# A float32r attention and gated feed-forward layer on one core: V projected for two heads at a time, residual rows kept partly in DRAM

## The chip, the cores and the metric

The kernel runs on one core of a Trainium2 chip. The metric is the device time of one execution in microseconds (us); lower is better. TensorE (PE) multiplies, VectorE (DVE), ScalarE (ACT) and GpSimd (POOL) work element by element, and SyncE (SP) issues most of the DMAs; ACT issues the rest. Each engine takes its own instructions strictly in the order in which they are written, and waits on semaphores of the others.

## The reference

```python
x = L0_attn_x                       # (4, 1024, 256)
q, k, v = x @ Wq + bq, x @ Wk + bk, x @ Wv + bv     # 16 heads of 128; q scaled by 128 ** -0.5
q, k = rotary(q), rotary(k)
attn = softmax(where(causal, -max, q @ k.T))
x = layernorm(x + (attn @ v) @ Wo + bo)
gate = silu((x @ w_gate) * s_gate); up = (x @ w_up) * s_up      # int8 weights, 1024 wide
x = layernorm(x + ((gate * up) @ w_down) * s_down)
```

## The kernel before

Every float32 operand of a product is kept as two float32r parts, high and low, and a product is the sum of three: high x high, high x low, low x high. So each operand costs a copy on ACT that makes the high part, and a subtraction on DVE or POOL that makes the low part (the helper `sub`, L582, on DVE, and the helper `copy`, L402, on ACT).

The work is a sequence of 64 heads (4 batches of 16). `run(n, par, ...)` writes out the time line of head `n`; `par` is 0 for even heads and 1 for odd ones, and picks the halves A or B of the double buffers. A time line has eight slots, `s` = 0 to 7. Slot `s` computes the scores of query rows `s` (L823), masks them and takes the maximum on DVE (L670), and exponentiates on ACT (L527). Slots 0 to 3 also project Q and K of head n + 1 in four chunks of 512 columns (L866), which ACT copies out (L535), DMAs swap (L283), POOL and DVE rotate (L347, L699, L646), and ACT and POOL split (L402, L358). Every even head's slots 2 and 3 and every odd head's slots 1 and 2 carry an output projection (L903), which DVE adds to the residual rows in `resid` (L692).

Probabilities are transposed on PE (L833), and the transposed block is split by ACT and DVE into `PT` before `attend` multiplies it with V (L848 to L850). The twelve steps k of a head are spread over its slots: steps 8 to 11 over its own slots 4 to 7 and the next head's slot 0, and steps 0 to 7, whose probabilities come from slots 4 to 7, over the next head's slots 0 to 4. The transposes of steps 0 and 1 are in slot 0, and wait for the exponential of the previous head's slot 7. After step 7 DVE normalises the output from bank `O` (`norm_o`, L627).

V of head n + 1 is projected in slots 4 to 7 of head n by `v_pair`, one pair of 128-row tiles each, into bank `PJ`. A tile takes four products: two 256 columns wide, in which the high part of x meets both parts of Wv, and two 128 columns wide. ACT copies the high half (L402), DVE subtracts it (L582 into `v_rest`) and adds the cross products (L638). In slots 4 to 7 ACT's order is the V copy, the copy of `PT`, the exponential; DVE's is the mask, `norm_o` in slot 4, the two V operations, the low part of `PT`, the rotation's sum (slots 4 and 5).

`resid` holds the rows of all four batches. Behind the last head comes the feed-forward stage in eight groups of 512 rows (`group`, L774, L969), of which six are in a loop.

Of the kernel before, what the change touches and what calls it, by code (L numbers as in the profile page):

```python
# [27 lines left out]
H, D = 16, 128  # L28
# [16 lines left out]
def layer(nc, x_rows, x_cols, w_heads, bias_qk, bias_v, wo_heads, bias_o, wg8, wu8, wd8, s_gate, s_up,  # L45
# [7 lines left out]
    def sem(name):  # L53
# [3 lines left out]
    recip_d = nc.dram_tensor("recip_d", (2, GQ), F32).ap()  # L57

# [3 lines left out]
    w_raw = sb("w_raw", [P, 3, KT, P])  # L62
    wo_raw = sb("wo_raw", [P, 2, DIM])

    W = [sb(f"W{s}", [P, 3, 2, KT, P], F32R) for s in "AB"]
# [8 lines left out]
    resid = sb("resid", [P, B * NT, DIM])  # L74
# [5 lines left out]
    v_rest = sb("v_rest", [P, 2, P])  # L80
# [30 lines left out]
    v_psum = PJ[:, :].rearrange("p (t a d) -> p t a d", t=2, a=2)  # L111
# [3 lines left out]
    W_in, x_first, x_in = sem("W_in"), sem("x_first"), sem("x_in")  # L115
    WO_in = sem("WO_in")
# [6 lines left out]
    maxed, pt_lo, cos_done, rot_done, v_sub, v_lo, o_norm, recip_ok, added = (  # L123
        sem(n) for n in ("maxed", "pt_lo", "cos_done", "rot_done", "v_sub", "v_lo", "o_norm", "recip_ok", "added"))
# [25 lines left out]
    def n_w(m, q):  # L150
        return 3 * m + (q + 1)

    def n_x(b, half):
        return b * 2 + (half + 1)

# [17 lines left out]
    def timelines(e, run):  # L173


        run(-1, 1, False, False, True, False)
        run(0, 0, True, False, True, False)
        run(1, 1, True, True, True, False)
        with e.Fori(1, PAIRS - 1) as it:
            run(it * 2, 0, True, True, True, True)  # L180
            run(it * 2 + 1, 1, True, True, True, True)
        run(HEADS - 2, 0, True, True, True, True)
        run(HEADS - 1, 1, True, True, False, True)
        run(HEADS, 0, False, True, False, True)

# [3 lines left out]
    def w_piece(n, s):  # L189
        return s - (4 if isinstance(n, int) and n < 0 else 1)  # L190
# [19 lines left out]
    def sequence_timelines(e, run):  # L210


        run(-1, 1, False, False, True, False)
        run(0, 0, True, False, True, False)
        run(1, 1, True, True, True, False)
        with e.Fori(1, H // 2 - 1) as it:
            run(it * 2, 0, True, True, True, True)
            run(it * 2 + 1, 1, True, True, True, True)
        with e.Fori(0, B - 1) as b:
            last = b * H + (H - 2)  # L220
            run(last, 0, True, True, True, True, b + 1)
            run(last + 1, 1, True, True, True, True, b + 1)
            with e.Fori(1, H // 2) as it:
                first = b * H + it * 2 + (H - 2)
                run(first, 0, True, True, True, True)
                run(first + 1, 1, True, True, True, True)
        run(HEADS - 2, 0, True, True, True, True)
        run(HEADS - 1, 1, True, True, False, True)
        run(HEADS, 0, False, True, False, True)


    flat_v = [v[:, :, :, :].rearrange("p a t d -> p (a t d)") for v in V]

    ffn_w = [xT[:, a, :, :].rearrange("p t n -> p (t n)") for a in range(2)] + [flat_v[0]]
    x1T = [t.rearrange("p (a t q) -> p a t q", a=2, t=KT)
           for t in (flat_v[1], OT[0][:, :, :].rearrange("p a n -> p (a n)"))]
# [19 lines left out]
    def groups(e, run):  # L256

        run(0, 0, True, True)
        with e.Fori(0, (FG - 2) // 2) as it:
            run(it * 2 + 1, 1, False, True)  # L260
            run(it * 2 + 2, 0, False, True)
        run(FG - 1, 1, False, False)

    with nc.Block() as block:  # L264

        @block.sync
        def _(sp):
# [9 lines left out]
            def run(n, par, own, prev, project, out_proj, next_x=None):  # L277
                for s in range(8):
# [6 lines left out]
                    if isinstance(n, int) and n == 0 and s == 6:  # L285
                        for b in range(B):
                            sp.dma_start(resid[:, b * NT:(b + 1) * NT, :], x_rows[b]).then_inc(resid_in, 16)
# [761 lines left out]
```

## Time and profile before

| | |
|---|---|
| median of 3 runs | 2173.8 us (2173.39 to 2177.66) |
| the profiled execution | 2175.21 us, of which 2173.4 us is the span of its instructions |
| mean granted TensorE clock over the span | 0.988 |
| PE, DVE, ACT, POOL busy | 2089.3, 1750.5, 1416.5, 1304.1 us |
| DMA | 150.27 MB, mean 69 GB/s |
| loads of all residual rows, at head 0 | 4 of 1024 KB, median 11.3 us to landing |
| loads of x for batches 1 to 3 | 3 of 1024 KB, median 5.2 us to landing |

Busy time is the time in which an engine worked on an instruction. For PE the ends of matmuls are modelled and neighbours overlap, so a busy PE can hide short waits: the distance between the starts of neighbours tells more. A wait of an engine is shown with the instruction that ended it.

### The profile page before, as it was taken

How to read it: one execution, taken by the hardware profiler on the slowest of the kernel's cores; microseconds unless marked ns; L12 is line 12 of the kernel's file. 1: busy time of each engine (PE TensorE's matmuls, PEld its weight loads, DVE VectorE, ACT ScalarE, POOL GpSimd, SP SyncE). 2: the span in 40 equal slices, each digit the busy share in tenths (PEclk: the TensorE clock that was granted, in tenths of full speed). 3: DMA queues.
4: the chain of work that ended last, by engine and by line, in shares of the span. 5: the costliest groups of instructions: out<-in, count | busy, mean ns of one | idle time of the engine just before them, and what ended most of it. 6: DMA issues, size and time to landing. Idle time of an engine off the chain costs nothing. (4 is left out here: it accounts for less than half of the span.)

```text
span 2173.4 us, 49354 instructions
## 1 busy us (share of the span) xinstructions
PE 2089.3 (96%) x13136; PEld 1860.5 (86%) x13136; DVE 1750.5 (81%) x3547; ACT 1416.5 (65%) x3230; POOL 1304.1 (60%) x1080
## 2 busy tenths in 40 slices
PE   6999999999999999999999999999999999979997
PEld 5888888888888888888888888888888888868886
DVE  5788888888888888888888888888888888865776
ACT  4676666676666666666667666676666776654543
POOL 4566656676666666576666666675666666524554
PEclk8999999999999999999999999999999999988999
DMA  4432223233232332333222233323232223310000
GB/s 115 148 73 68 72 73 73 64 86 75 73 73 73 67 69 70 73 92 70 68 68 73 73 73 70 84 72 73 74 69 68 68 73 73 80 25 1 29 19 29
DMA packets 99871, 150.27 MB, mean 69 GB/s; under 512 B 31216, under 2 KB 35824, under 8 KB 99312
## 3 DMA queue, kind: packets, MB, share of 16 engines
q1 hardware_dynamic: 85856, 115.82, 22.2%
q10 hardware_dynamic: 13968, 33.95, 5.7%
q14 instruction: 33, 0.27, 0.1%
q8 instruction: 14, 0.23, 0.0%
HBM read 78.15 MB, written 4.46 MB: 38 GB/s over the span
## 5 line engine op out<-in xcount | busy, mean ns | idle before, releaser
L582 DVE TENSOR_TENSOR PT<-TP,PT 128x512 fp32r<-128x512 f32 (+3 forms) x768 | 421.3, 552 | 210.0 <-ACT PT L402 206.7
L527 ACT ACTIVATE prob<-prob,neg_max 128x128 f32<-128x128 f32 (+7 forms) x512 | 397.8, 777 | 288.4 <-DVE neg_max L670 280.4
L402 ACT ACTIVATE PT<-TP 128x512 fp32r<-128x512 f32 (+3 forms) x768 | 361.4, 489 | 90.3 <-PE TP L833 80.6
L670 DVE CUSTOM_DVE_ANT_0 prob<-S,mask_row 128x128 f32<-128x128 f32 (+7 forms) x512 | 380.7, 744 | 27.1 <-PE TP L833 12.4
L347 POOL TENSOR_TENSOR swap<-swap,sin_t 128x512 f32<-128x512 f32 x256 | 350.3, 1368 | 82.7 <-DMA swap<-proj 80.4
L833 PE MATMUL TP<-ident,prob 128*128 128x128 f32 x2304 | 369.4, 274 | 0.7 <-ACT prob L527 0.7
L833 PEld LDWEIGHTS TP<-ident,prob 128*128 128x128 f32 x2304 | 283.1, 141 | 55.5 <-ACT prob L527 1.1
L646 DVE TENSOR_TENSOR rot<-rot,swap 128x512 f32<-128x512 f32 x256 | 286.3, 1119 | 7.6 <-POOL swap L347 7.2
L358 POOL TENSOR_TENSOR QKB<-rot,QKB 128x512 fp32r<-128x512 f32 x128 | 171.8, 1342 | 196.1 <-ACT QKB L402 196.1
L358 POOL TENSOR_TENSOR QKA<-rot,QKA 128x512 fp32r<-128x512 f32 x128 | 182.4, 1425 | 169.1 <-ACT QKA L402 168.4
L823 PE MATMUL S<-QKB 128*128 128x512 f32 (+4 forms) x1152 | 261.2, 353 | 1.3 <-DVE resid L692 1.3
L823 PE MATMUL S<-QKA 128*128 128x512 f32 (+4 forms) x1152 | 259.9, 352 | 1.1 <-ACT proj L535 1.1
L535 ACT ACTIVATE proj<-S,bias_m 128x512 f32<-128x512 f32 x256 | 173.8, 679 | 91.1 <-DVE rot L646 89.1
L866 PE MATMUL S<-xT,WA 128*128 128x512 f32 x768 | 200.7, 398 | 8.9 <-DVE xT L582 8.9
L823 PEld LDWEIGHTS S<-QKB 128*128 128x128 f32 x1152 | 187.4, 190 | 17.9 <-issue 1.5
L823 PEld LDWEIGHTS S<-QKA 128*128 128x128 f32 x1152 | 186.9, 189 | 18.1 <-issue 1.7
L866 PE MATMUL S<-xT,WB 128*128 128x512 f32 x768 | 201.3, 397 | 0.0
L337 POOL TENSOR_TENSOR norm_o<-norm_o,bias_o_m 128x512 f32<-128x512 f32 x128 | 134.2, 1049 | 96.3 <-ACT OTA L483 67.3
L699 DVE TENSOR_TENSOR rot<-proj,cos_t 128x512 f32<-128x512 f32 x256 | 178.7, 698 | 8.0 <-ACT proj L535 8.0
L627 DVE TENSOR_TENSOR norm_o<-O,recip_b 128x512 f32<-128x512 f32 x128 | 140.4, 1097 | 40.9 <-PE O L850 40.9
L866 PEld LDWEIGHTS S<-xT,WA 128*128 128x128 f32 x768 | 140.9, 190 | 34.6 <-issue 8.9
L848 PE MATMUL O<-PT,VA 128*128 128x512 f32 (+3 forms) x384 | 141.5, 369 | 27.5 <-DVE PT L582 27.5
(107 smaller groups left out, 4722.9 us busy)
## 6 DMA issues: line engine op xcount, KB each, us to landing
swap<-proj SPq DMA_DIRECT2D x512, 128.0 KB, 2.3
recip_b<-recip_d SPq DMA_DIRECT2D x128, 256.0 KB, 3.6
w_raw<-in_w_heads ACTq DMA_DIRECT2D x65, 384.0 KB, 3.1
wo_raw<-in_wo_heads ACTq DMA_DIRECT2D x32, 256.0 KB, 3.3
resid<-in_x_rows SPq DMA_DIRECT2D x4, 1024.0 KB, 11.3
out<-resid SPq DMA_DIRECT2D x8, 512.0 KB, 3.0
x_raw<-in_x_cols SPq DMA_DIRECT2D x3, 1024.0 KB, 5.2
recip_d<-recip SPq DMA_DIRECT2D x128, 2.0 KB, 1.8
```

What stands on the lines that cost most here:

```text
L347: nc.gpsimd.tensor_tensor(swap[:, c % 2, :], swap[:, c % 2, :], sin_t[:, half], ALU.mult).then_inc(sin_done, 1)
L358: nc.gpsimd.tensor_tensor(q[:, c % 2, 1, half], rot[:, c, :], q[:, c % 2, 0, half].bitcast(F32), ALU.subtract).then_inc(rot_lo, 1)
L402: copy = lambda o, i: nc.scalar.activation(o, i, ACT.Copy)
L527: nc.scalar.activation(row, row, ACT.Exp, bias=neg_max[:, s:s + 1], scale=-1.0, accum_out=row_sum[:, s:s + 1]).then_inc(exped, 1)
L535: nc.scalar.activation(proj[:, c % 2, :], S[c % 2][:, GQ:], ACT.Identity, bias=bias_m[:, m_par, c % 2:c % 2 + 1], scale=SCALE if c % 2 == ...
L582: sub = lambda o, a, b: nc.vector.tensor_tensor(o, a, b, ALU.subtract)
L646: nc.vector.tensor_tensor(rot[:, c, :], rot[:, c, :], swap[:, c % 2, :], ALU.add).then_inc(rot_done, 1)
L670: nc.vector.tensor_tensor_reduce(row_view(prob[g][:, prob_at[g][i]:prob_at[g][i] + cols], s), score_view(S[s % 2], s), row_view(mask_row[: ...
L699: nc.vector.tensor_tensor(rot[:, c, :], proj[:, c % 2, :], cos_t[:, half], ALU.mult).then_inc(cos_done, 1)
L823: last = mm(S[s % 2][:, z * GQ:z * GQ + b - a], QK[par][:, 0, part_q, s * P:(s + 1) * P], QK[par][:, 1, part_k, a:b], start=(part_q, part_ ...
L833: last = nc.tensor.transpose(TP[k % 2][:, i * P:(i + 1) * P], prob[g][:, prob_at[g][i] + j * P:prob_at[g][i] + (j + 1) * P], ident[:, :])
L866: last = mm(S[c % 2][:, GQ:], W[nxt][:, c % 2, pw, t, :], xT[:, px, t, half], start=i == 0 and t == 0, stop=i == 2 and t == KT - 1)
```

## The change

`WV` holds the weights of two heads side by side, and `V` the values of two. V of heads n + 2 and n + 3 (n even) is now projected in slots 4 and 6 of head n and of head n + 1, one group of two row tiles each; a tile takes six products of 256 columns, and all three parts are summed in PSUM. One 512-column copy and one 512-column subtraction a group then make the two parts. In slot 4 the group stands ahead of the steps 6 and 7 on PE; on ACT its copy stands behind the exponential of the slot, and on DVE its subtraction stands behind the low part of `PT`. W is split in slots 2 and 3 instead of 1 to 3, and `WV` in slot 1 of even heads. `resid` holds two batches: one in work and a neighbour; finished rows go to `attn_d` in DRAM (1 MB a batch) and the next ones are loaded in their place, at the heads around a change of batch, where the split of the next x has moved too, to slots 2 and 5 of one head. For the feed-forward stage the rows come back into `resid` and the `prob` buffers. The attention loops are written out by four heads instead of two, and the feed-forward groups without a loop.

```diff
-    w_raw = sb("w_raw", [P, 3, KT, P])
+    w_raw = sb("w_raw", [P, 2, KT, P])
+    wv_raw = sb("wv_raw", [P, 2, KT, P])
+    WV = sb("WV", [P, 2, KT, 2, P], F32R)
-    V = [sb(f"V{s}", [P, 2, NT, P], F32R) for s in "AB"]
+    V = [sb(f"V{s}", [P, 2, NT, 2 * P], F32R) for s in "AB"]
-    resid = sb("resid", [P, B * NT, DIM])
+    resid = sb("resid", [P, 2 * NT, DIM])
+    attn_d = nc.dram_tensor("attn_d", (B, P, NT, DIM), F32).ap()
...
+    def v_group(n, par, s):
+        if isinstance(n, int) and n < 0:
+            return s - 4 if s >= 4 else None
+        return {4: 2 * par, 6: 2 * par + 1}.get(s) if makes_v(n) else None
...
@@ PE
-                        mm(v_psum[:, t2, :, :], xT[:, 0, 0, tok], w[:, :, 0, :], start=True, stop=False)
-                        for t in range(KT):
-                            mm(v_psum[:, t2, 0, :], xT[:, 1, t, tok], w[:, 0, t, :], start=False, stop=False)
-                        last = mm(v_psum[:, t2, :, :], xT[:, 0, 1, tok], w[:, :, 1, :],
-                                  start=False, stop=True)
+                        for z, (px, pw) in enumerate(((0, 0), (0, 1), (1, 0))):
+                            for t in range(KT):
+                                last = mm(v_psum[:, t2, :], xT[:, px, t, tok],
+                                          WV[:, pw, t, :, :].rearrange("p h c -> p (h c)"),
+                                          start=z == 0 and t == 0, stop=z == 2 and t == KT - 1)
...
+                    i = v_group(n, par, s)
+                    if s == 4 and i is not None:
+                        values(i)
                     if s == 4 and prev:
-                        attend(n, 6, nxt)
-                        attend(n, 7, nxt)
-                    if s == 4 and project:
-                        v_pair(0)
+                        attend(n, 6, nxt, before)
+                        attend(n, 7, nxt, before)
                     if s >= 4 and own:
                         transposes(s + 4)
-                    if s > 4 and project:
-                        v_pair(s - 4)
+                    if s > 4 and i is not None:
+                        values(i)
@@ ACT
-                    if s >= 4 and project:
-                        v = s - 4
-                        act.wait_ge(v_made, n_four(m, v))
-                        wait(act, attended, n_step(n, 7))
-                        copy(V[nxt][:, 0, 2 * v:2 * v + 2, :],
-                             v_psum[:, :, 0, :]).then_inc(v_hi, 1)
                     if s >= 4 and own:
                         probs_hi(n, s + 4)
                     if own and s >= 4:
                         softmax(n, s)
+                    i = v_group(n, par, s)
+                    if i is not None:
+                        act.wait_ge(v_made, n_v(n, par, i))
+                        if par == 0:
+                            wait(act, attended, n_step(n, 7))
+                        copy(V[1 - vb][:, 0, 2 * i:2 * i + 2, :], v_psum).then_inc(v_hi, 1)
...
+                    if next_x is not None and par == 0 and s == 0:
+                        act.wait_ge(added, n_added(n - (H - 2), 3))
+                        act.dma_start(attn_d[bass.ds((next_x + 2) & 3, 1)].rearrange("b p t c -> (b p) t c"),
+                                      half_resid(next_x)).then_inc(attn_out, 16)
+                    if next_x is not None and par == 1 and s == 3:
+                        act.wait_ge(attn_out, next_x * 16)
+                        act.dma_start(half_resid(next_x), x_rows[bass.ds(next_x, 1)].rearrange("b p t c -> (b p) t c")
+                                      ).then_inc(resid_in, 16)
+                    if isinstance(n, int) and n == HEADS - 2 and s == 6:
+                        act.wait_ge(attn_out, 16 * B)
+                        act.dma_start(resid[:, 0:NT, :], attn_d[0]).then_inc(attn_in, 16)
@@ DVE
-                    if s >= 4 and project:
-                        v = s - 4
-                        dve.wait_ge(v_hi, n_four(m, v))
-                        wait(dve, v_lo, n_four(m, v) - 1)
-                        tiles = slice(2 * v, 2 * v + 2)
-                        sub(v_rest[:, :, :], v_psum[:, :, 0, :], V[nxt][:, 0, tiles, :].bitcast(F32)
-                            ).then_inc(v_sub, 1)
-                        dve.wait_ge(v_sub, n_four(m, v))
-                        nc.vector.tensor_tensor(V[nxt][:, 1, tiles, :], v_rest[:, :, :], v_psum[:, :, 1, :],
-                                                ALU.add).then_inc(v_lo, 1)
                     if s >= 4 and own:
                         probs_lo(n, s + 4)
+                    i = v_group(n, par, s)
+                    if i is not None:
+                        dve.wait_ge(v_hi, n_v(n, par, i))
+                        tiles = slice(2 * i, 2 * i + 2)
+                        sub(V[1 - vb][:, 1, tiles, :], v_psum, V[1 - vb][:, 0, tiles, :].bitcast(F32)).then_inc(v_lo, 1)
```

PE, slot 4 of an even head in the middle of the sequence, before: the last scores, steps 6 and 7, V (PJ), the transposes of step 8.

```order
L823 MATMUL S<-QKA 128x320 x6
L845 REGISTER_ALU
L848 MATMUL O<-PT,VB 128x256
L849 MATMUL O<-PT,VB 128x256
L850 MATMUL O<-PT,VB 128x256
L848 MATMUL O<-PT,VB 128x128
L849 MATMUL O<-PT,VB 128x128
L850 MATMUL O<-PT,VB 128x128
L874 REGISTER_ALU
L878 MATMUL PJ<-WB,xT 128x256
L880 MATMUL PJ<-WB,xT 128x128 x2
L881 MATMUL PJ<-WB,xT 128x256
```

The same place of the change:

```order
L894 MATMUL S<-QKA 128x320 x6
L206 ISA
L945 ISA
L946 ISA
L951 MATMUL PJ<-WV,xT 128x256 x12
L916 REGISTER_ALU
L919 MATMUL O<-PT,VB 128x256
L920 MATMUL O<-PT,VB 128x256
L921 MATMUL O<-PT,VB 128x256
L919 MATMUL O<-PT,VB 128x128
L920 MATMUL O<-PT,VB 128x128
L921 MATMUL O<-PT,VB 128x128
```

V stood behind the six products of steps 6 and 7 and now stands ahead of them, with twelve products instead of eight. Slot 6 has the same twelve, and slots 5 and 7 none.

ACT, slot 6 of an even head, before: V (VB), the high part of PT, the exponential, a copy of the rotated rows.

```order
L402 ACTIVATE VB<-PJ 128x256
L517 REGISTER_ALU
L402 ACTIVATE PT<-TP 128x256
L524 REGISTER_ALU
L527 ACTIVATE prob,row_sum<-prob,neg_max 128x896
L402 ACTIVATE QKB<-rot 128x512
```

The same slot of the change:

```order
L447 ACTIVATE PT<-TP 128x256
L601 REGISTER_ALU
L604 ACTIVATE prob,row_sum<-prob,neg_max 128x896
L447 ACTIVATE VB<-PJ 128x512
L447 ACTIVATE QKB<-rot 128x512
```

The V copy has moved from ahead of the exponential to behind it.

DVE, slot 6 and the start of slot 7 of an even head, before: the mask, the two V operations, the low part of PT, the mask of slot 7.

```order
L670 ISA prob,neg_max<-S,mask_row 128x896
L670 ISA neg_max 128x1
L582 TENSOR_TENSOR v_rest<-PJ,VA 128x256
L638 TENSOR_TENSOR VA<-v_rest,PJ 128x256
L678 REGISTER_ALU
L582 TENSOR_TENSOR PT<-TP,PT 128x256
L619 REGISTER_ALU
L670 ISA prob,neg_max<-S,mask_row 128x1024
```

The same stretch of the change:

```order
L741 ISA prob,neg_max<-S,mask_row 128x896
L741 ISA neg_max 128x1
L749 REGISTER_ALU
L656 TENSOR_TENSOR PT<-TP,PT 128x256
L710 REGISTER_ALU
L656 TENSOR_TENSOR VB<-PJ,VB 128x512
L695 REGISTER_ALU
L741 ISA prob,neg_max<-S,mask_row 128x1024
```

One V operation is left of two, and it stands directly ahead of the mask of slot 7.

## Rows read from the trace of the kernel before

**Rows 1.** Page, part 1: busy us, share of the span, instructions.

```profile
PE 2089.3 (96%) x13136; PEld 1860.5 (86%) x13136; DVE 1750.5 (81%) x3547; ACT 1416.5 (65%) x3230; POOL 1304.1 (60%) x1080
```

**Rows 2.** Waits of PE, 100 to 1880 us: total, times, longest.

```profile
PE O L848 <- DVE PT L582: 19.8, 28, 1.0
PE PJ L878 <- DVE VA L638: 8.1, 22, 0.6
```

**Rows 3.** Timeline, PE, an odd and an even head: start, duration, count, idle before.

```profile
1012.38 1.06 PE L833 MATMUL TP<-ident,prob 128*128 128x128 f32 x8
...
1029.58 0.39 PE L848 MATMUL O<-PT,VA 128*128 128x256 f32 x1 [0.70 <-DVE PT L582]
...
1042.74 1.07 PE L833 MATMUL TP<-ident,prob 128*128 128x128 f32 x8
...
1059.10 0.28 PE L848 MATMUL O<-PT,VB 128*128 128x256 f32 x1
...
1059.74 0.33 PE L878 MATMUL PJ<-WB,xT 128*128 128x256 f32 x1
...
1060.71 0.60 PE L833 MATMUL TP<-ident,prob 128*128 128x128 f32 x4
...
1071.81 1.06 PE L833 MATMUL TP<-ident,prob 128*128 128x128 f32 x8
```

**Rows 4.** Timeline, PE, one V tile and the steps behind it.

```profile
1009.56 0.28 PE L878 MATMUL PJ<-WB,xT 128*128 128x256 f32 x1
...
1010.02 0.28 PE L848 MATMUL O<-PT,VA 128*128 128x256 f32 x1
1010.14 0.28 PE L849 MATMUL O<-PT,VA 128*128 128x256 f32 x1
```

**Rows 5.** Timeline, DVE, slots 4 to 7 of the even head.

```profile
1060.28 1.10 DVE L627 TENSOR_TENSOR norm_o<-O,recip_b 128x512 f32<-128x512 f32 x1
...
1062.13 0.68 DVE L582 TENSOR_TENSOR PT<-TP,PT 128x512 fp32r<-128x512 f32 x1
...
1062.73 0.68 DVE L646 TENSOR_TENSOR rot<-rot,swap 128x512 f32<-128x512 f32 x1
...
1063.42 0.93 DVE L670 CUSTOM_DVE_ANT_0 prob<-S,mask_row 128x768 f32<-128x768 f32 x1
...
1065.06 0.55 DVE L582 TENSOR_TENSOR PT<-TP,PT 128x384 fp32r<-128x384 f32 x1
...
1066.13 1.08 DVE L670 CUSTOM_DVE_ANT_0 prob<-S,mask_row 128x896 f32<-128x896 f32 x1
...
1068.75 1.23 DVE L670 CUSTOM_DVE_ANT_0 prob<-S,mask_row 128x1024 f32<-128x1024 f32 x1 [0.40 <-PE TP L833]
```

**Rows 6.** Timeline, ACT, same head, and the end of step 11.

```profile
1061.85 0.82 ACT L527 ACTIVATE prob<-prob,neg_max 128x640 f32<-128x640 f32 x1
...
1067.26 1.04 ACT L527 ACTIVATE prob<-prob,neg_max 128x896 f32<-128x896 f32 x1
...
1070.09 1.15 ACT L527 ACTIVATE prob<-prob,neg_max 128x1024 f32<-128x1024 f32 x1
...
1071.70 0.28 PE L850 MATMUL O<-PT,VA 128*128 128x128 f32 x1
...
1072.17 1.11 DVE L627 TENSOR_TENSOR norm_o<-O,recip_b 128x512 f32<-128x512 f32 x1 [0.82 <-PE O L850]
```

**Rows 7.** Groups by shape, 400 to 1700 us: busy us, mean ns, idle before.

```profile
L402 ACT ACTIVATE PT<-TP 128x512 fp32r<-128x512 f32 x259 | 147.6, 596 | 30.7 <-PE TP L833 24.2
```

**Rows 8.** Timeline, DVE, a rotation sum of the odd head.

```profile
1033.38 1.25 DVE L646 TENSOR_TENSOR rot<-rot,swap 128x512 f32<-128x512 f32 x1
```

**Rows 9.** Timeline, PE in the last head; busy by stretch: PE, PEld, DVE, ACT, POOL, PEclk, DMA.

```profile
1926.33 0.38 PE L848 MATMUL O<-PT,VA 128*128 128x256 f32 x1 [2.17 <-DVE PT L582]
...
1926.00:1932.00 6.00, 5.67 (x27) 5.06 (x28) 5.53 (x11) 3.35 (x6) 2.09 (x2) 0.72 0.05 16
```

**Rows 10.** Waits, 50 to 75 us: total, times, longest.

```profile
PE O L848 <- DVE PT L582: 3.6, 1, 3.6
```

More of the change, by code:

```diff
@@ L189, in w_piece @@
     def w_piece(n, s):
-        return s - (4 if isinstance(n, int) and n < 0 else 1)
+        return s - (4 if isinstance(n, int) and n < 0 else 2)
     def output_of(n, par, s, out_proj):
@@ L227, in sequence_timelines, with four @@
[L227 to L234, printed above, removed]
+        def four(first, next_x=None):
+            run(first, 0, 0, True, True, True, True)
+            run(first + 1, 1, 0, True, True, True, True)
+            run(first + 2, 0, 1, True, True, True, True, next_x)
+            run(first + 3, 1, 1, True, True, True, True, next_x)
@@ new lines, in sequence_timelines @@
+        run(-1, 1, 1, False, False, True, False)
+        run(0, 0, 0, True, False, True, False)
+        run(1, 1, 0, True, True, True, False)
+        run(2, 0, 1, True, True, True, True)
+        run(3, 1, 1, True, True, True, True)
+        with e.Fori(1, H // 4 - 1) as it:
+            four(it * 4)
+        with e.Fori(0, B - 1) as b:
+            four(b * H + (H - 4), b + 1)
+            with e.Fori(1, H // 4) as it:
+                four(b * H + it * 4 + (H - 4))
+        run(HEADS - 4, 0, 0, True, True, True, True)
@@ L254, in layer, with rows, groups @@
     DOWN_AFTER = {0: [-2], 1: [-1], 2: [], 3: [0, 1], 4: [2], 5: [3], 6: [4], 7: [5]}
[L256 to L262, printed above, removed]
+    late_rows = [p[:, 0:tiles * DIM].rearrange("p (t c) -> p t c", c=DIM) for p, tiles in ((prob[1], 12), (prob[0], 4))]
+    def rows(g, t, count=1):
+        if g < 2:
+            held = resid[:, g * TPG + t:g * TPG + t + count, :]
+        elif g < 5:
+            held = late_rows[0][:, (g - 2) * TPG + t:(g - 2) * TPG + t + count, :]
+        elif g == 5:
+            held = late_rows[1][:, t:t + count, :]
+        else:
+            held = resid[:, (g - 4) * TPG + t:(g - 4) * TPG + t + count, :]
+        return held.rearrange("p a c -> p (a c)")
+    def groups(run):
+        for g in range(FG):
+            run(g, g % 2, g == 0, g < FG - 1)
     with nc.Block() as block:
@@ L285, in run @@
                     if isinstance(n, int) and n == 0 and s == 6:
-                        for b in range(B):
+                        for b in range(2):
                             sp.dma_start(resid[:, b * NT:(b + 1) * NT, :], x_rows[b]).then_inc(resid_in, 16)
@@ L492, in run @@
                         copy(QK[nxt][:, c % 2, 0, half], rot[:, c, :]).then_inc(rot_hi, 1)
-                    if n_has(n, project) and w_piece(n, s) in range(3):
+                    if n_has(n, project) and w_piece(n, s) in range(2):
                         w_high(n + 2, par, w_piece(n, s))
+                    if par == 0 and s == 1 and own and makes_v(n):
+                        wv_high((n >> 1) + 1)
+                    if par == 0 and s == 5 and own and makes_v(n) and n_has(n + 2 if isinstance(n, int) else n, True):
+                        load_wv(n)
                     if s == 5 and n_has(n, project):
@@ L576, in group @@
                             x1T_high(g + 1, 1 - par, t)
-            groups(act, group)
+            groups(group)
         @block.vector
@@ L836, in transposes, with attend @@
                     last.then_inc(transposed, 1)
-                def attend(nn, k, who):
+                def attend(nn, k, who, buf):
                     g, j, c0 = step(k)
@@ L914, in run @@
                         output(s, *made)
+                    before = vb if par else 1 - vb
                     if prev and s == 0:
-                        attend(n - 1, 11, nxt)
+                        attend(n - 1, 11, nxt, before)
                         transposes(0)
```

201 lines of the change are left out of this document (112 added, 89 removed).

## The prediction

> **What bounds the kernel now.** I read the page first: PE is busy 96% of the span and DVE 81% [rows 1]. A busy PE can hide waits, so I looked next at who waits for whom in the steady stretch from 100 to 1880 us: PE stands still for only 28 us of 1780, nearly all of it ahead of `attend`, for DVE [rows 2]. Last I read the timeline of two neighbouring heads [rows 3]. The first transposes of slot 0 (step 0, "T0") start at 1012.38, 1042.74 and 1071.81: an odd head takes 30.36 us and an even one 29.07, 29.7 in the mean. Between them PE's instructions follow each other closely, but for the 0.70 us in slot 4 of the odd head, where step 6 waits for the low part of `PT`. So the PE is the bound, but by a narrow margin: what follows it on DVE and ACT is just in time. In the even head DVE goes from one instruction to the next from `norm_o` at 1060.28 to the mask of slot 7 at 1068.75, with an idle time of 0.40 us in those 8.5 us [rows 5]. The reader should see two chains of nearly one length in slots 4 to 7, and only PE's in slots 0 to 3.
>
> **What is taken from PE.** A V tile takes 0.46 us of PE (1009.56 to 1010.02), and products of 256 columns follow each other at 0.12 (1010.02 to 1010.14) [rows 4]. Before, a head has four groups of two tiles, about 1.0 us each (0.97 from 1059.74 to 1060.71 in [rows 3]), so 3.9. After, it has two groups of twelve products, 12 x 0.12 = 1.4, so 2.8. PE has about 1.1 us a head less to do. The odd head's 0.70 us goes too, because V now stands ahead of step 6 and fills it. If PE alone set the pace, this would be (1.1 + 0.35) x 61 heads = 88 us.
>
> **What the new order costs.** I follow the even head from the start of step 6, 1059.10 [rows 3], by distances of rows. Slots 0 to 3 hold no V; from T0 at 1042.74 to 1059.10 PE is the bound as before, 16.36 us.
> 1. V first: 1059.10 + 1.4 = 1060.5; steps 6 and 7 take 0.64 (1059.10 to 1059.74), so step 8's transposes start at 61.15, and step 7's last product at 61.05.
> 2. `norm_o` starts 0.47 behind the start of such a last product (1071.70 to 1072.17 [rows 6]): 61.52, where it was at 1060.28. DVE used to do it while PE projected V. It and its 1.1 us end at 62.6.
> 3. The exponential of slot 4 starts 1.14 behind the transposes (1060.71 [rows 3] to 1061.85 [rows 6]): 62.30, and takes 0.82. Only then comes the V copy, 0.60 for 512 columns [rows 7]: to 63.7. DVE does the low part of step 8, 0.6 (1062.13 to 1062.73 [rows 5]), to 63.2, and waits 0.6 for the copy. I give the new subtraction the same 0.6, since it reads PSUM and SBUF in the same shape: 63.8 to 64.4.
> 4. The rotation's sum and the reciprocal take 0.69 (1062.73 to 1063.42): the mask of slot 5 starts at 65.1, 1.7 later than before. It, the low part and the second rotation's sum take 0.85 + 1.07 (1065.06 to 1066.13) [rows 5]: the mask of slot 6 starts at 67.0.
> 5. The exponential of slot 6 starts 1.13 behind its mask (1066.13 [rows 5] to 1067.26 [rows 6]), and takes 1.04; the V copy 0.6; then the subtraction, 69.9 to 70.5. DVE has only the mask and a short low part, 1.4 us, to do in these 2.9, and stands idle for 1.5. Before, ACT made the V copy ahead of the exponential, and this wait wasn't there.
> 6. The mask of slot 7 stands behind it in DVE's queue: 70.5, where it was at 1068.75. Its exponential starts 1.34 later (1068.75 [rows 5] to 1070.09 [rows 6]) and takes 1.15; with 0.15 to release T0, that is 73.15. Before, T0 was at 1071.81, and V in slot 7 covered this exponential; now PE has come to the end of step 11 sooner and waits.
>
> So a head takes 16.36 + 14.05 = 30.4 us, the odd head as well, since its chain has the same parts. Against 29.7 that is +0.7, and + 0.7 x 61 = +43 us. DVE does 1.0 us a head less and loses about 2 us waiting for ACT: the saving of PE isn't used.
>
> **What else moves.** The four groups before head 0 are longer and each waits for the one before; I take +2. Two of the four residual loads are gone from head 0, behind which PE waited 3.6 us at 50 to 75 us [rows 10]: up to -3.6, I take -2. At the three batch changes there are 2 MB more traffic and POOL's long split among the rotations; the trace doesn't show it, and between nothing and that same 3.6 us each I take 1.5, so +4. The first batch's rows come back from DRAM just ahead of the last head's first sums, where DVE is in the way: +0 to +3.6, I take 1. The feed-forward stage has the same work without its loop, and its loads have the last head's time as cover: 0. A split of `WV` and one of `W` fewer on POOL and ACT lie in their idle time: 0; without that cover it would be 0.6 a pair. Sum: +5. The profiled execution, 2175.2, becomes 2223; the median of the runs is 1.4 lower: 2222. I round to **2220**.
>
> **Rivals.**
> *Faster, PE keeps the pace (30%).* My chain adds thirteen distances; an error of 0.1 in most of them, or V copies that ACT gets to sooner, takes the 1.5 us of step 5 away. Then what holds PE is its own work and only the release of T0: the distance from the mask of slot 7 to T0 was 3.06 and PE covered it; with V gone from slot 7 it lacks 0.6. A head is then 29.7 - 1.1 - 0.35 + 0.6 = 28.9, or -0.8 x 61 + 5 = -44: 2130, and 2095 where T0 doesn't wait. For it speaks that DVE has 1 us less work a head; against it, that nothing in the order lets ACT copy V before the exponential. It decides once DVE's waits for V copies are below 1.3 us a head in sum.
> *No change (5%).* Half of the waits: 2170 to 2178.
> *Slower, DVE and POOL also collide (12%).* The odd head's rotation sum took 1.25 us [rows 8] where the even head's took 0.68 [rows 5], with a POOL multiplication beside it. In the new chain the sums stand directly between V and the masks; at 0.57 more in each head: +35, so 2255. The Trainium skill (SBUF — State Buffer, the part on the ports) says that a DVE operation with two inputs in SBUF and a GpSimd operation lock each other out for a whole instruction; by that rule each sum is exposed to a coin toss, and the pair of rows agrees with it.
> *Slower, the clock falls (3%).* Behind a PE wait of 2.17 us in the last head the granted clock of the next 6 us is 0.72 [rows 9]: part at 1.2 instead of 2.4 GHz. Two waits, at step 11 and T0, add up to 1.9 us a head in my chain. At one such fall in each head, 6 x 0.28 = 1.7 us, it is 2320.
> *As forecast (50%)*: 2190 to 2240.
>
> **How the numbers follow.** The range reaches from 2110, which leaves out a quarter of the faster case (8%), to 2250, which leaves out the clock and most of the collision (10%). The forecast's own range is 2190 to 2240. A measurement of this kernel tells a difference over 0.2%. Faster: 30% and a little of the rest, 0.32. Same: 0.05. Slower: 0.63.
>
> **What would show it.** Right: PE waits for DVE ahead of step 11 and for ACT's exponential ahead of T0 in nearly every head, some 100 us in sum where it was 28; DVE's V subtraction waits for ACT's copy, most in slot 6; T0 to T0 is 30.4 in both kinds of head; V groups of 1.4 us. Wrong: distances of 29 or less, DVE without such waits, the mask of slot 5 less than 1 us later than before against step 6. What would make it wrong is above all step 5: if DVE is ahead enough of PE that exponential and copy find it still busy, or if ACT's queue is short of work there.

## The result, and the profile after

The changed kernel takes 2251.0 us (median of 4 runs, 2249.4 to 2256.4) and the kernel before, on the same chip, 2175.7 (4 runs, 2173.4 to 2178.4): a ratio of 1.035, 95% interval 1.0327 to 1.0373. Slower was forecast, by 44 us; it is 75, and 2251 lies 1 us above the range. The profiled execution has a span of 2247.6 us, 74.2 more than before's 2173.4.

The page of the changed kernel, part 1 (busy time, share, instructions) and two queues of part 3, answers to [rows 1]:

```profile
PE 2083.4 (93%) x12624; PEld 1812.3 (81%) x12624; DVE 1605.4 (71%) x3163; ACT 1390.7 (62%) x3070; POOL 1288.7 (57%) x1048
...
q8 instruction: 70, 1.15, 0.2%
q14 instruction: 156, 1.28, 0.2%
```

Every engine has less to do, and all of them wait more. The q rows are the queues that bring instructions: 226 packets now (70 + 156), 2.4 MB; the kernel before had 47, 0.5 MB. That comes back below.

Waits of PE and of DVE from 100 to 1950 us (total, times, longest), against [rows 2]:

```profile
PE O L919 <- DVE PT L656: 57.2, 69, 1.7
PE TP L904 <- ACT prob L604: 33.7, 57, 0.6
PE S L894 <- issue: 8.7, 2, 4.4
...
DVE VA L656 <- ACT VA L447: 56.5, 60, 1.4
DVE VB L656 <- ACT VB L447: 52.8, 59, 1.3
```

PE waits for 106 us in all, 5.9 of it in a row not shown. DVE waits 109 us for ScalarE's copies of V, 1.8 us a head. The timeline of PE in one head, slots 4 to 7 and the start of the next (start, duration, count, idle before), against [rows 3]:

```profile
316.77 1.60 PE L951 MATMUL PJ<-WV,xT 128*128 128x256 f32 x12
318.21 0.28 PE L919 MATMUL O<-PT,VA 128*128 128x256 f32 x1
...
318.85 0.63 PE L904 MATMUL TP<-ident,prob 128*128 128x128 f32 x4
...
323.06 1.67 PE L951 MATMUL PJ<-WV,xT 128*128 128x256 f32 x12
...
329.53 0.33 PE L919 MATMUL O<-PT,VA 128*128 128x128 f32 x1 [0.70 <-DVE PT L656]
...
330.68 0.55 PE L904 MATMUL TP<-ident,prob 128*128 128x128 f32 x3 [0.60 <-ACT prob L604]
```

DVE in the same head, against [rows 5], and ACT, against [rows 6]:

```profile
319.06 1.07 DVE L703 TENSOR_TENSOR norm_o<-O,recip_b 128x512 f32<-128x512 f32 x1
...
321.45 0.69 DVE L656 TENSOR_TENSOR VB<-PJ,VB 128x512 fp32r<-128x512 f32 x1 [0.60 <-ACT VB L447]
...
322.74 0.93 DVE L741 CUSTOM_DVE_ANT_0 prob<-S,mask_row 128x768 f32<-128x768 f32 x1
...
324.66 1.08 DVE L741 CUSTOM_DVE_ANT_0 prob<-S,mask_row 128x896 f32<-128x896 f32 x1
...
327.44 0.69 DVE L656 TENSOR_TENSOR VB<-PJ,VB 128x512 fp32r<-128x512 f32 x1 [1.27 <-ACT VB L447]
328.05 1.21 DVE L741 CUSTOM_DVE_ANT_0 prob<-S,mask_row 128x1024 f32<-128x1024 f32 x1
```

```profile
320.01 0.82 ACT L604 ACTIVATE prob<-prob,neg_max 128x640 f32<-128x640 f32 x1
320.73 0.19 ACT L604 ACTIVATION_READ_ACCUMULATOR prob<-prob,neg_max 128x1 f32 x1
320.82 0.59 ACT L447 ACTIVATE VB<-PJ 128x512 fp32r<-128x512 f32 x1
...
325.79 1.05 ACT L604 ACTIVATE prob<-prob,neg_max 128x896 f32<-128x896 f32 x1
326.74 0.19 ACT L604 ACTIVATION_READ_ACCUMULATOR prob<-prob,neg_max 128x1 f32 x1
326.83 0.58 ACT L447 ACTIVATE VB<-PJ 128x512 fp32r<-128x512 f32 x1
...
329.30 1.15 ACT L604 ACTIVATE prob<-prob,neg_max 128x1024 f32<-128x1024 f32 x1 [1.21 <-DVE neg_max L741]
```

Read the last three fences as one chain: the exponential of slot 6 to 326.84, the copy of V to 327.41, the subtraction at 327.44, the mask of slot 7 at 328.05, its exponential at 329.30, T0 at 330.68.

The other surcharges show when the span is cut at every T0. Busy time by stretch (length; PE, PEld, DVE, ACT, POOL; granted clock, DMA share, GB/s): a steady head, one behind a jump back of the loop by four heads, the two heads of the first batch change, one at a jump of the outer loop (the loop over batches), and the head behind the second batch change:

```profile
300.40:330.68 30.28, 28.94 (x181) 25.40 (x181) 22.21 (x45) 19.48 (x45) 16.66 (x15) 1.00 0.29 70
268.74:300.40 31.66, 29.30 (x180) 25.34 (x181) 22.50 (x47) 20.47 (x47) 20.34 (x17) 1.00 0.27 67
452.19:487.25 35.06, 29.88 (x180) 25.42 (x181) 26.46 (x45) 21.81 (x49) 25.18 (x19) 1.00 0.40 121
487.25:521.42 34.17, 30.97 (x180) 26.68 (x181) 24.12 (x45) 19.47 (x45) 16.97 (x15) 0.95 0.36 93
858.29:893.32 35.03, 30.57 (x180) 26.98 (x181) 22.81 (x44) 20.52 (x48) 18.88 (x16) 0.92 0.27 62
1023.45:1055.36 31.91, 30.55 (x180) 26.65 (x181) 22.97 (x45) 20.69 (x47) 19.39 (x17) 0.95 0.28 67
```

With all 63 such stretches of both kernels the 74.2 us fall into parts. 61 heads at 30.35 instead of a mean of 29.78: +35. Six heads at the three batch changes, 207.1 us against 6 x 30.35, and the heads behind the second and the third change, 31.91 and 31.98 at clocks of 0.95 and 0.94: +28. Seven heads behind jumps back of the inner loops, 31.7 to 31.8 each: +10. Two at the outer loop's jumps, 35.0 and 34.7: +9. Start and first head: -4. Last heads and feed-forward: -4.

The expectations below speak of nine heads behind jumps and 13 us. Two of their nine are the heads behind batch changes: the order of the loops has no jump back there, PE waits no longer in them than in a steady head (0.6 us at T0, 0.7 to 0.8 at step 11), and it is the clock that is lower.

### The profile page after: what moved, and what is told of

Same layout as the page of the kernel before. It is cut to its first block and busy times, and to the rows that moved or that the text cites. A ratio compares the mean times of both kernels' runs of the same rounds, so it can differ in the third digit from the quotient of the medians.

```text
span 2247.6 us, 46236 instructions
## 1 busy us (share of the span) xinstructions
PE 2083.4 (93%) x12624; PEld 1812.3 (81%) x12624; DVE 1605.4 (71%) x3163; ACT 1390.7 (62%) x3070; POOL 1288.7 (57%) x1048
## 5 line engine op out<-in xcount | busy, mean ns | idle before, releaser
L904 PE MATMUL TP<-ident,prob 128*128 128x128 f32 x2304 | 375.0, 277 | 36.3 <-ACT prob L604 36.3
L717 DVE TENSOR_TENSOR rot<-rot,swap 128x512 f32<-128x512 f32 x256 | 244.4, 955 | 11.5 <-POOL swap L386 11.3
L951 PE MATMUL PJ<-WV,xT 128*128 128x256 f32 x1536 | 210.8, 287 | 8.9 <-DVE VA L656 8.9
L951 PEld LDWEIGHTS PJ<-WV,xT 128*128 128x128 f32 x1536 | 194.7, 191 | 9.7 <-DVE VA L656 9.6
L919 PE MATMUL O<-PT,VB 128*128 128x512 f32 (+3 forms) x384 | 150.3, 391 | 48.0 <-DVE PT L656 46.9
```

The costliest lines, as they stand in the source:

```text
L717: nc.vector.tensor_tensor(rot[:, c, :], rot[:, c, :], swap[:, c % 2, :], ALU.add).then_inc(rot_done, 1)
L904: last = nc.tensor.transpose(TP[k % 2][:, i * P:(i + 1) * P], prob[g][:, prob_at[g][i] + j * P:prob_at[g][i] + (j + 1) * P], ident[:, :])
L951: last = mm(v_psum[:, t2, :], xT[:, px, t, tok], WV[:, pw, t, :, :].rearrange("p h c -> p (h c)"), start=z == 0 and t == 0, stop=z == 2 an ...
```

## The experiments

The variants ran on other chips than the changed kernel. The kernel before took 2169.9 to 2172.3 us beside them and 2175.7 beside the changed kernel, so where a variant's whole time is compared with the changed kernel's 2251.0, some 6 us are open. Heads within the traces don't suffer from this.

**1. Which wait sets the steady head.** In `v_copy_first` ScalarE copies V ahead of the exponential:

```diff
                     if s >= 4 and own:
                         probs_hi(n, s + 4)
-                    if own and s >= 4:
-                        softmax(n, s)
                     i = v_group(n, par, s)
                     if i is not None:
...
+                    if own and s >= 4:
+                        softmax(n, s)
```

> The changed kernel with one move: on ScalarE, in slots 4 and 6, the V copy stands between the high part of PT and the exponential, not behind the exponential. Theory A (steady heads are held by the chain mask, exponential, V copy, V subtraction, next mask): VectorE's waits for V copies, 109 us in 100 to 1950 us, fall below 30 us; the release of slot 0's transposes comes about 1.4 us a head sooner, so a steady head takes 28.9 instead of 30.3 us, and the whole about 2165 us (2150 to 2185). Rival B (the longer heads come from the amount of work, or from the loops and DMAs, not from this order): within 10 us of the changed kernel's 2251.

Measured: 2193.4 us, ratio to the kernel before 1.0107 (1.0085 to 1.0128), 58 less than the changed kernel, or 53 by the ratios. That is still 8 us above the range of 2150 to 2185: the order was worth less than expected, since the heads are 29.06 and about 29.7 and not 28.9. Not one wait of DVE for a V copy is left, and PE's two waits (100 to 1900 us) are down from 89.8 us to 49.5:

```profile
PE O L919 <- DVE PT L656: 28.9, 27, 3.4
PE TP L904 <- ACT prob L604: 20.6, 57, 0.5
```

So the order on ScalarE is what makes the steady head long. What holds the odd heads at 29.7 no run takes apart.

In `v_slots_5_7` the V groups stand in slots 5 and 7:

```diff
-        return {4: 2 * par, 6: 2 * par + 1}.get(s) if makes_v(n) else None
+        return {5: 2 * par, 7: 2 * par + 1}.get(s) if makes_v(n) else None
```

> The changed kernel with the V groups in slots 5 and 7 instead of 4 and 6. Theory A: V in slot 7 again covers the exponential of that slot, so TensorE's wait ahead of slot 0's transposes (0.6 us a head) goes; but VectorE's subtraction of slot 7 now stands ahead of the mask of slot 0 and norm_o and waits for exponential and copy there, some 1.4 us. In sum between 29.7 and 30.3 us a steady head, 2215 to 2250 us. Rival (TensorE's uncovered wait alone is the cause): 29.1 us a head and about 2180.

Measured: 2259.1, ratio 1.0402 (1.0382 to 1.0422). This missed. Steady heads are 29.95 and 30.83, the same mean as before the edit, and heads behind jumps went from 31.7 to 35 and more. DVE (100 to 1900 us) waits longer for V, and now also for its own instructions:

```profile
DVE VA L656 <- ACT VA L447: 71.7, 59, 1.3
DVE VB L656 <- ACT VB L447: 68.2, 56, 1.3
...
DVE prob L741 <- issue: 25.7, 9, 3.0
```

`v_5_7_copy_first` has both edits.

> Both of the other two edits: V groups in slots 5 and 7, V copy ahead of the exponential. Theory A: neither chain is left; steady heads at TensorE's own pace, 28.4 to 28.8 us, whole 2135 to 2165 us. Rival B (order doesn't matter): 2240 or more.

Measured: 2150.8, ratio 0.991 (0.9893 to 0.9926), heads 28.22 and 29.01: faster than the kernel before. The slots are worth 43 us once the copy is first, and cost 8 us (11 by the ratios) while it isn't.

**2. The loops.** The change also writes each engine's loop by four heads instead of two, since two buffers of V for pairs of heads take turns. DVE's body grew from 178 to 324 instructions, ScalarE's from 164 to 323, PE's from 452 to 861 (a load and its matmul counted once, waits on semaphores not counted). DVE and PE had one plain loop before; now they too have the outer loop, which holds two such bodies. `before_four_head_loop` writes this plain loop out by four heads, for PE and DVE of the kernel before:

```diff
-        with e.Fori(1, PAIRS - 1) as it:
-            run(it * 2, 0, True, True, True, True)
-            run(it * 2 + 1, 1, True, True, True, True)
+        run(2, 0, True, True, True, True)
+        run(3, 1, True, True, True, True)
+        with e.Fori(1, HEADS // 4 - 1) as it:
+            four(it * 4)
+        run(HEADS - 4, 0, True, True, True, True)
+        run(HEADS - 3, 1, True, True, True, True)
```

> The kernel before with one change: the attention loops of TensorE and VectorE are written out by four heads instead of two; the work and its order are the same. Theory C (a loop body of four heads no longer stays in VectorE's instruction memory; each jump back costs a fetch): 14 jumps at 1.4 us, so about 2195 us (2185 to 2205), VectorE standing idle about 2 us ahead of the mask of slot 0 once in four heads. Rival D (the 1.4 us once in four heads in the changed kernel come from its weight loads): 2174 us, no change.

Measured: 2220.6, ratio 1.0221 (1.0204 to 1.0238): +48 us from not one different instruction of work, twice what was expected. `before_dve_four` and `before_pe_four` do it for one engine:

> The kernel before with VectorE's loop alone written by four heads a pass; all other engines keep two. With both VectorE's and TensorE's loops by four heads it took 2220.6 against 2172.3 us, 3.9 us more in every fourth head. Theory: VectorE's jump back is what costs (it stood idle there in the changed kernel): 2205 to 2225. Rival: TensorE's body is the one that is too long: 2172 within 5.

> The kernel before with TensorE's loop alone by four heads. With VectorE's alone it took 2221.2, with both 2220.6. Theory C: TensorE's loop costs nothing, 2170 within 3. Rival: its body too has a jump that is not covered, 2180 or more.

Measured: DVE alone 2221.2, ratio 1.023 (1.0213 to 1.0247), all of it. PE alone 2171.0, ratio 1.0001 (0.9991 to 1.001), nothing. In `before_dve_four` every fourth head takes 33.1 instead of 29.07. The rows are: the stretch of an even head, of one behind a jump, then DVE's first mask behind the jump, PE, and DVE's waits for such masks from 100 to 1880 us, 13 for 13 jumps:

```profile
335.63:364.67 29.04, 29.04 (x190) 26.25 (x190) 24.32 (x50) 20.21 (x50) 19.23 (x17) 1.00 0.29 68
271.91:304.99 33.08, 30.93 (x191) 27.55 (x190) 24.24 (x52) 20.44 (x50) 19.11 (x17) 0.95 0.24 60
...
274.12 0.29 DVE L689 CUSTOM_DVE_ANT_0 prob<-S,mask_row 128x128 f32<-128x128 f32 x1 [2.86 <-PE S L842]
...
276.88 0.50 PE L867 MATMUL O<-PT,VB 128*128 128x512 f32 x1 [2.15 <-DVE PT L601]
...
DVE prob L689 <- PE S L842: 37.3, 13, 3.0
```

DVE stands for 2.86 us with its scores long there; PE then waits 2.15, and its busy time grows by 1.9 at a granted clock of 0.95. The Trainium skill (Runtime: NRT & Kernel Launch, Instruction fetch mechanics) says that a taken branch whose target isn't among the two pages of instructions at hand makes the engine fetch it first; these runs agree, and their price is 2.9 us of DVE. The packets of the queues that bring instructions agree too: 47 in the kernel before, 117 with DVE's long loop, 57 with PE's; and the 226 of the changed kernel are 63 in `after_short_loops` below, where the feed-forward stage is written out as well.

In the changed kernel the same place is this, on DVE behind a jump back, and PE at a jump of the outer loop ("issue": it waited for nothing that the profile shows):

```profile
269.58 0.29 DVE L741 CUSTOM_DVE_ANT_0 prob<-S,mask_row 128x128 f32<-128x128 f32 x1 [2.05 <-PE TP L904]
...
889.43 0.90 PE L894 MATMUL S<-QKA 128*128 128x128 f32 x3 [4.43 <-issue]
```

`after_short_loops` finds V's buffer by a register, so that all but PE can loop by two heads; PE has one plain loop by four.

```diff
-    V = [sb(f"V{s}", [P, 2, NT, 2 * P], F32R) for s in "AB"]
+    V = sb("V", [P, 4, NT, 2 * P], F32R)
...
+        a = V[:, bass.ds(buf * 2 + part, 1), tiles, cols]
+    def buf_of(n, other=0):
+        return (n // 2 + other) % 2 if isinstance(n, int) else ((n >> 1) + other) & 1
...
-            sequence_timelines(dve, run)
+            timelines(dve, run)
```

> The changed kernel with its loops shortened: VectorE, ScalarE, GpSimd and SyncE go by two heads per pass as before the change (the buffer of V is then found by a register), TensorE by four heads, but in one plain loop instead of a loop over batches around two copies of the four heads. In the changed kernel the head behind each jump back takes 31.7 us instead of 30.3 (nine of them, 13 us in all) and the two heads at the jumps of the outer loop 35 us (some 9 us in all). Theory C (a jump back in the long loop bodies of VectorE costs time, and the outer loop's far jumps too): those 20 us go, 2228 to 2235 us, and all heads outside the batch changes take 30.3. Rival (TensorE's own long body costs it): the two outer jumps' 9 us go, the 31.7 stay, about 2240. Rival that the loops are no cause: 2250.

Measured: 2274.3, ratio 1.0475 (1.0458 to 1.0493), 39 us above the expected range. The jumps' surcharges are gone, at the outer loop too (30.9), but the register has a price that I had left out: in the trace the subtraction starts 0.48 us behind the end of ScalarE's copy, where it was 0.04. Here are ScalarE's copy and DVE's subtraction:

```profile
330.16 0.59 ACT L480 ACTIVATE V<-PJ 128x512 f32 x1
...
331.23 0.69 DVE L689 TENSOR_TENSOR V<-PJ,V 128x512 f32 x1 [1.05 <-ACT V L480]
```

Steady heads take 30.9 and 31.0, and eight others 32.4 to 32.5 at a clock of 0.95. `after_dve_short` shortens DVE's loop and keeps PE's plain one, and `after_dve_long` gives `after_short_loops` DVE's long loop back, with a fixed buffer:

> The changed kernel with VectorE's loop alone by two heads; ScalarE, GpSimd and SyncE keep the changed kernel's loops and fixed buffers, TensorE one plain loop of four heads. VectorE finds the buffer of V by a register, which in after_short_loops put some 0.45 us between the end of ScalarE's copy and VectorE's subtraction and brought the steady head from 30.3 to 30.9 us. Theory C (VectorE's jump back in a long body is what costs): no head behind a jump back stands out by 1.4 us or more; steady heads 30.5 to 30.9, 2245 to 2265 in all. Rival (the jumps of the other engines count): the 31.7 heads stay behind every fourth head.

> after_short_loops (2274.3: all engines but TensorE by two heads, V's buffer by a register on VectorE and ScalarE), with VectorE's loop by four heads again, as in the changed kernel, and its buffer of V fixed. It tells the price of VectorE's long loop apart from ScalarE's: in after_dve_short ScalarE's instruction behind its jump back came 1.06 us late and the head took 32.1 instead of 30.9. Theory: each engine's long loop costs 1.0 to 1.5 us per jump by itself, and they overlap in the changed kernel; here every fourth head is 1.0 to 1.5 us (with a fall of the clock, up to 3) above the others, and the others are 30.3 to 30.6 without the register on VectorE: 2245 to 2265. Rival (only ScalarE's jump counts in the changed kernel): no head behind a jump stands out, 2235 to 2245.

Measured: 2283.2, ratio 1.0519 (1.0498 to 1.0541), 18 us above the expected range, and 2240.3, ratio 1.0331 (1.0311 to 1.035), 5 us below it. With DVE short, nine heads behind jumps still take 32.1 to 32.4 instead of 30.9, and the head behind each of them takes 32.4 at a clock of 0.95, which the expectation had not counted; the row is ScalarE's first instruction behind its own jump. With DVE long and ScalarE short, two neighbouring stretches, the second behind a jump:

```profile
277.10 0.40 ACT L670 ACTIVATE prob<-prob,neg_max 128x128 f32<-128x128 f32 x1 [1.06 <-issue]
...
240.86:271.14 30.28, 28.98 (x181) 25.45 (x181) 22.32 (x42) 19.51 (x45) 16.66 (x15) 1.00 0.30 71
271.14:302.71 31.57, 29.31 (x181) 25.36 (x181) 22.25 (x47) 20.46 (x47) 20.10 (x17) 1.00 0.27 67
```

DVE's long loop alone costs 1.0 to 1.2 us a jump here, ScalarE's alone 1.2 to 1.5 besides the fall of the clock behind it, and both together 1.4: they overlap. `after_dve_long` is 11 us below the changed kernel (4 by the ratios). In its trace the two heads at the outer loop's jumps fall from 35.0 and 34.7 to 30.3, which is 9 us: PE's outer loop is gone. In `after_dve_short`, where ScalarE keeps its outer loop, they take 30.9 like their neighbours, so it is PE's that cost.

**3. The batch changes.** `no_row_traffic` moves one row instead of 1 MB out and 1 MB in:

```diff
-                        act.dma_start(attn_d[bass.ds((next_x + 2) & 3, 1)].rearrange("b p t c -> (b p) t c"),
-                                      half_resid(next_x)).then_inc(attn_out, 16)
+                        act.dma_start(attn_d[bass.ds((next_x + 2) & 3, 1), 0:1, 0:1].rearrange("b p t c -> (b p) t c"),
+                                      resid[0:1, bass.ds((next_x & 1) * NT, 1), :]).then_inc(attn_out, 16)
```

> The changed kernel without the 1 MB of residual rows written out and the 1 MB loaded at each of the three batch changes: one row of one partition moves instead, so that every wait is still there. At the end the late rows come from x_rows and not from where the rows were put, so the output leaves the attention result out of the residual of batches 0 to 2. Theory E1 (the traffic delays the swaps and rotations at the batch changes, which cost 27 us more over six heads than before): 20 to 27 us go, 2225 to 2230. Rival E2 (the x split, which the change moved, crowds VectorE there, traffic is hidden): 2250 within 4, and the batch-change heads stay at 34 to 35 us.

`no_x_split` cuts GpSimd's two subtractions for the next batch's x to 16 columns:

```diff
-                        nc.gpsimd.tensor_tensor(halves(xT, 1, half), halves(x_raw, None, half),
+                        one = slice(half * GQ, half * GQ + 16)
+                        nc.gpsimd.tensor_tensor(xT[:, 1, 0, one], x_raw[:, 0, one],
```

> The changed kernel with GpSimd's two long subtractions per batch change (the low halves of the next batch's x, 128 x 1024, 2.4 to 2.9 us each) cut to 16 columns each, with all waits kept; the low half of x of batches 1 to 3 is left out but for those columns, so the output is another. Theory E2: these two stand in GpSimd's queue ahead of the rotation's multiplications and splits of the same head, and cost the first head of each change 2 to 4 us: 2236 to 2243, and the first head of each pair at 31 to 33 instead of 35.1, 34.9 and 34.9. Rival (the traffic alone makes the surcharge): 2250 within 4.

> no_row_traffic and no_x_split together, with what both leave out. no_row_traffic took 2237.2. If traffic and split are the whole surcharge of the batch changes, the six heads come down to 30.3 to 31 and the time to 2222 to 2230. Rival: a third cause (the 2 MB load of x itself, or ScalarE's two long copies of x), then the six heads stay 1 us or more above 30.4 and the time is 2231 to 2237.

Measured, with the six heads at the changes (the changed kernel: 2251.0 and 207.1): 2237.2 and 193.0; 2242.1 and 194.2; both 2229.3 and 187.8. The first lies 7 us above its range, the other two within theirs. Their ratios are 1.0299 (1.0281 to 1.0316), 1.0339 (1.0317 to 1.0361) and 1.0273 (1.0255 to 1.029). So each alone is worth 13 to 14 us of these heads and both 19. With the head behind each change, which is at 30.4 in all three places once both are left out, it is 16, 13 and 22 of the 28 us. The whole time of `no_x_split` gains less, 9 us (2 by the ratios): in its trace 6 us come back at the start, in the last heads and behind them, where the edit changes nothing. The stretches of the first change in the kernel without either:

```profile
454.95:485.66 30.71, 29.10 (x181) 25.40 (x181) 21.67 (x45) 22.25 (x49) 20.27 (x19) 1.00 0.40 105
485.66:516.70 31.04, 29.37 (x181) 25.55 (x181) 23.67 (x45) 19.51 (x45) 17.10 (x15) 1.00 0.28 69
```

Of the 28 us, 6 stay open; two of the second heads there have a clock of 0.95 and take 32.3. In the changed kernel GpSimd's row reads so at the first change:

```profile
464.97 1.30 POOL L386 TENSOR_TENSOR swap<-swap,sin_t 128x512 f32<-128x512 f32 x1 [2.43 <-DMA swap<-proj]
466.21 2.86 POOL L391 TENSOR_TENSOR xT<-x_raw,xT 128x1024 fp32r<-128x1024 f32 x1
469.04 1.17 POOL L411 TENSOR_TENSOR WA<-w_raw,WA 128x256 fp32r<-128x256 f32 x1
470.18 1.29 POOL L386 TENSOR_TENSOR swap<-swap,sin_t 128x512 f32<-128x512 f32 x1
```

Both work on the same stage. The traffic makes the swap's transfer late: over the two heads GpSimd waits 11.0 us for it, 12.0 without the split, but 5.8 without the traffic. The split, 2.86 us in GpSimd's queue, holds the next swap's multiplication. `before_row_traffic` adds the same traffic to the kernel before:

```diff
+                    if next_x is not None and par == 0 and s == 0:
+                        act.wait_ge(added, n_added(n - (H - 2), 3))
+                        act.dma_start(attn_d[bass.ds((next_x + 2) & 3, 1)].rearrange("b p t c -> (b p) t c"),
...
+                    if next_x is not None and par == 1 and s == 3:
```

> The kernel before, with 1 MB of residual rows written to DRAM and read back at each of the three batch changes, at the same places as in the changed kernel. no_row_traffic was 14 us faster than the changed kernel, with the heads at the batch changes at 32.9 instead of 35.1 and 34.2. Theory E1: the traffic costs some 3.5 us per batch change here as well, 2178 to 2186. Rival (before has room for it; only the tighter changed kernel feels it): 2170 to 2175.

Measured: 2180.4, ratio 1.004 (1.0026 to 1.0054), +9 us, as expected; the six heads +7. The same traffic costs the changed kernel 14 in these heads.

**4. The version the experiments point to.** `best_short_loops` is `v_5_7_copy_first` with the loops of `after_short_loops`; `best_dve_short` has the short loop on DVE alone, ScalarE's buffer fixed.

> The version with the V groups in slots 5 and 7 and ScalarE's V copy ahead of its exponential (which took 2150.8 us), now with the same short loops. In v_5_7_copy_first steady heads take 28.2 and 29.0. Theory C: the heads behind the jumps lose their surcharge, some 15 to 30 us off, 2120 to 2138. Rival (loops no cause): 2150.

> The version with V groups in slots 5 and 7 and the V copy ahead of the exponential, with VectorE's loop alone by two heads and ScalarE's V copy at a fixed buffer (best_short_loops, with all short and a register in both, took 2128.8). Theory: VectorE's loop gives all of the loop gain; ScalarE's register address cost up to 0.2 us per group. 2115 to 2130. Rival (ScalarE's, GpSimd's and SyncE's jumps matter too): 2135 to 2150.

Measured: 2128.8, ratio 0.9813 (0.9797 to 0.9829), and 2127.4, ratio 0.9796 (0.978 to 0.9813). PE is 96% busy again, as in [rows 1]. Neighbouring heads of the second, the first of them behind a jump of ScalarE:

```profile
258.44:287.61 29.17, 28.58 (x183) 25.35 (x182) 22.20 (x44) 20.53 (x48) 20.07 (x16) 1.00 0.32 73
287.61:316.60 28.99, 28.45 (x183) 25.39 (x182) 22.23 (x44) 19.61 (x46) 17.74 (x15) 1.00 0.29 73
316.60:344.82 28.22, 28.22 (x183) 25.41 (x182) 23.28 (x44) 20.41 (x49) 19.65 (x16) 1.00 0.28 75
```

The two come out alike because one price stands for another. In `best_dve_short` the heads behind ScalarE's jumps take 29.0 to 29.3 instead of 28.2, so DVE's loop does not give all of the gain, though that was expected. In `best_short_loops` no head stands out there, but that kind of head takes 28.3 to 28.7: the registers cost up to 0.5 us, less than the 0.6 they cost where the subtraction stands on the chain. So V for two heads at once can be worth 44 us on this kernel; in the place that the change gives it, it costs 75.

## Why the prediction was right or wrong

**The bound and what is taken from PE: right.** A V group took 1.44 to 1.51 us (316.77 to 318.21, 323.06 to 324.57) against 1.4. By the distances between starts V takes 2.95 us a head (1.44 + 1.51), where its four groups took 3.98 in the even head of [rows 3]: 1.0 less, against 1.1.

**The six steps: right, to 0.15 us.** Distances from the first V product: step 8's transposes 2.05 forecast, 2.08 measured; `norm_o` 2.42 and 2.29; exponential of slot 4 3.20 and 3.24; subtraction 4.7 and 4.68; mask of slot 5 6.0 and 5.97; of slot 6 7.9 and 7.89; second subtraction 10.8 and 10.67; mask of slot 7 11.4 and 11.28; T0 14.05 and 13.91. Slots 0 to 3 took 16.37 (300.40 to 316.77) against 16.36. Heads are 30.28 and 30.40, PE waits 91 us at the two places named, DVE waits for V in slot 6 most (1.27 against 0.60). `v_copy_first` shows that this is a cause: take the copy out of the chain and 53 to 58 us go.

**The size of that term: 8 us too large.** It was "Against 29.7 that is +0.7, and + 0.7 x 61 = +43 us". Two heads stood for 61 there; over all of them the mean before was 29.78 and after 30.35, so +35.

**"What else moves ... Sum: +5": the step that failed.** It measured +39.
- "At the three batch changes ... I take 1.5, so +4" measured +28. Its upper bound, 3.6 us a change, came from one wait at the start; the mechanism (traffic, and GpSimd's split among the rotations) was named, and no_traffic_no_x_split gives it 22 of the 28. A change costs 9.4 us, not 1.5: both of its heads pay, the second also by a clock of 0.95 or less, and behind two of the changes a third head by the clock alone.
- The loops had no term at all: +19 (seven jumps back of the inner loops 10, two of the outer loop 9). The listing of instructions shows the bodies grow from two heads to four, and I read only the order within a head. That the price exists is shown by before_dve_four. That a jump costs less in the changed kernel (1.4 against 4.0) I put down to the waits that stand beside it there anyway and to the clock, which stays at 1.00; this is argued only.
- Start, first head, last head and feed-forward: "+2", "-2", "+1" and "0" measured -8 together.

So 43 + 5 = 48 was forecast, and 35 + 47 - 8 = 74 came.

**The rivals.** *PE keeps the pace* failed for the reason given against it: ScalarE has no order in which V is copied first. Given one, the kernel goes that rival's way (28.9 forecast; 29.4 in v_copy_first, and 28.6 in best_dve_short with slots and loops moved as well). *DVE and POOL collide*: not more than before. The rotation's sums took 948 ns in the mean, where they took 1130 before, so some still take long, but fewer; that 2251 lies near this rival's 2255 is chance, for it came about in other ways. The rule of the Trainium skill named there isn't refuted by this, it just doesn't add a surcharge here. *The clock falls*: in part. In the changed kernel 9 of the 63 heads have a clock below 1.00, in the one before 2; length times what is missing sums to 19 us against 3. It fell in no steady head, but at the outer loop's jumps and behind one of them, in the second head of each batch change and behind two of them, and in the last head; so it is mostly part of the two terms above.

## What to carry to other kernels

Price the loop as well as the body: when a schedule's period doubles, so do the loop bodies, and an engine that was on time just so can pay at every jump back, as VectorE and ScalarE did here and TensorE only in its outer loop. Where a change adds an operation on one engine that another engine's next instruction waits for, look first at what stands ahead of it in the queue; here one exchange of two lines was worth 53 to 58 us. And a wait bounded by one row near the program's start says little of the steady stage, where each surcharge goes through every queue behind it.

## What the runs showed of the hardware that wasn't expected

- A loop body of 340 instructions on VectorE (before_dve_four) cost 2.9 us at a jump back and one of 178 nothing that shows; on ScalarE 323 cost 1.06 us (after_dve_short). TensorE's bodies of 861 (after) and 899 (before_pe_four) cost nothing, while its outer loop over two bodies of 861 cost 4.4 and 4.3 us at its two jumps. Waits on semaphores are not in these counts.
- An address held in a register, computed behind the wait, put 0.44 us more between a release and VectorE's start (after_short_loops), at 0.6 us a head.
- Small waits and the clock: the waits of a head don't tell its clock. In the changed kernel PE stands for 0.6 us at T0 and 0.6 to 0.8 at step 11 in steady heads at a clock of 1.00, and no longer in the two heads behind batch changes at 0.95 and 0.94, which take 1.5 us more. In after_short_loops it stands for 0.6 and 0.8 to 1.1; eight such heads have 0.95 and take 1.5 to 1.6 us more, and most have 1.00. Behind the wait of 2.15 us in before_dve_four the clock fell in each of the 13 such heads.
